# Attention without a turn back to tokens: two heads per column group, inverse sums spread by DMA, engine turns reordered

## The reference, cut to what matters

```python
x = x + L1_attn(layernorm(x), ...)        # x: 32 sequences, 256 tokens, 128 wide
# inside, HEADS = 16, HEAD_DIM = 8:
q = (h @ Wq.T + bq).reshape(b, s, 16, 8) * 8 ** -0.5
k = (h @ Wk.T + bk).reshape(b, s, 16, 8)
v = (h @ Wv.T + bv).reshape(b, s, 16, 8)
scores = einsum('bqhd,bkhd->bhqk', q, k)
probs  = softmax(scores, axis=-1)
out = einsum('bhqk,bkhd->bqhd', probs, v).reshape(b, s, 128)
return out @ Wo.T + bo
```

## Time and profile before

| | us |
|---|---|
| median of 3 runs (lowest, highest) | 1351.31 (1344.29, 1352.7) |
| the profiled execution, its own time | 1346.88 |
| its span in the trace | 1345.1 |
| attention phase: first M unit to last `add_y` | 633 to 1168 |
| PE, DVE, ACT, POOL busy over the whole span | 77%, 57%, 48%, 55% |
| DMA packets, MB | 92931, 104.74 |

### The profile page before, as it was taken

One profiled execution on the slowest core, in us unless ns is written; L12 is line 12 of the kernel. 1 busy time (PEld: TensorE's weight loads), 2 busy tenths in 40 slices (PEclk: granted clock), 3 DMA queues, 4 the chain that ended last, 5 costly groups with the idle time before them and its releaser, 6 DMA issues. The chain is left out here.

```text
span 1345.1 us, 31339 instructions
## 1 busy us (share of the span) xinstructions
PE 1032.9 (77%) x9288; PEld 732.2 (54%) x9289; DVE 763.8 (57%) x1576; ACT 647.5 (48%) x1294; POOL 745.8 (55%) x1517
## 2 busy tenths in 40 slices
PE   5688889568877776744899999999999999513455
PEld 4577777357854444432566666666666666302143
DVE  4466666363432222212677777777777777245982
ACT  4455555211212222212677777777777777402212
POOL 4455555245523333336667777777777775373312
PEclk9899999578999899985899999999999999856787
DMA  4700000301111111134333444444444443110000
GB/s 159 287 0 0 0 0 1 105 30 41 41 41 53 48 56 52 51 95 136 102 109 112 129 127 123 118 123 130 123 119 120 121 127 108 45 35 28 1 1 16
DMA packets 92931, 104.74 MB, mean 78 GB/s; under 512 B 11199, under 2 KB 76735, under 8 KB 92491
## 3 DMA queue, kind: packets, MB, share of 16 engines
q1 hardware_dynamic: 85530, 82.73, 21.6%
q0 software_dynamic: 5760, 11.68, 2.7%
q10 hardware_dynamic: 1584, 9.60, 1.8%
HBM read 62.48 MB, written 40.67 MB: 77 GB/s over the span
## 5 line engine op out<-in xcount | busy, mean ns | idle before, releaser
L1223 DVE TENSOR_REDUCE a_neg_max<-a_slot 128x4 f32<-128x1024 f32 x256 | 312.1, 1222 | 133.9 <-PE a_slot L1364 127.0
L1312 ACT ACTIVATE a_pT<-a_slot 128x1024 f32<-128x1024 f32 x256 | 257.8, 1020 | 83.3 <-PE a_slot L1378 78.4
L1378 PE MATMUL a_slot<-a_q_stack,a_k_stack 75*128 75x256 bf16 x1024 | 155.2, 274 | 17.7 <-ACT a_pT L1312 12.0
L1364 PE MATMUL a_slot<-a_k_stack,a_q_stack 72*128 72x256 bf16 x1024 | 157.5, 277 | 6.6 <-DMA a_k_stack<-part_dram 6.0
L661 POOL DMA_INDIRECT y_rows<-m_total,m_token x80 | 76.8, 960 | 137.3 <-ACT m_total L791 121.4
L1393 PE MATMUL a_ps_o<-a_pT,a_v_pad 128*32 128x256 f32 x2048 | 139.2, 385 | 0.0
L311 DVE TENSOR_TENSOR r_score<-ps_score,r_decay 128x512 f32<-128x512 f32 x128 | 85.0, 687 | 71.2 <-PE ps_score L442 67.8
L1364 PEld LDWEIGHTS a_slot<-a_k_stack,a_q_stack 72*128 72x128 bf16 x1024 | 90.8, 99 | 58.4 <-issue 31.0
L1378 PEld LDWEIGHTS a_slot<-a_q_stack,a_k_stack 75*128 75x128 bf16 x1024 | 92.3, 97 | 54.6 <-DVE a_neg_max L1223 41.3
L852 PE MATMUL m_banks<-expert_up,m_xeT 128*128 x160 | 82.9, 642 | 49.8 <-issue 39.4
L754 DVE COPY m_same<-m_banks 128x512 f32<-128x512 f32 x40 | 27.7, 692 | 140.7 <-PE m_banks L860 108.7
...
## 6 DMA issues: line engine op xcount, KB each, us to landing
...
part_dram<-a_part SPq DMA_DIRECT2D x64, 64.0 KB, 2.1
x_rows<-x SPq DMA_DIRECT2D x32, 128.0 KB, 3.6
```

Source lines behind the costliest of these rows:

```text
L1223: nc.vector.tensor_reduce(neg_max[:, p, half, t, g * UNIT:(g + 1) * UNIT], slots[SLOT_OF["m", j]][:], AX.X, ALU.max, negate=True).then_inc ...
L1312: nc.scalar.activation(pT[:, j % PT_RING], slots[SLOT_OF["e", j]][:], ACT.Exp).then_inc(e_read, 1)
L1364: ins = nc.tensor.matmul(slots[SLOT_OF["m", j]][:, q], q_stack[0:QK_ROWS, p, half, head, t * P:(t + 1) * P], k_stack[0:QK_ROWS, p, half, h ...
L1378: ins = nc.tensor.matmul(slots[SLOT_OF["e", j]][:, q], k_stack[0:EXP_ROWS, p, half, head, t * P:(t + 1) * P], q_stack[0:EXP_ROWS, p, half, ...
```

## The change

Heads 2j and 2j+1 share a column group of 32 columns: each has 16 (v, ones, zeros), and all four matmuls (two heads, two token tiles) add into one PSUM area, so that all 16 heads fit in the 128 partitions of two halves. ACT copies both halves in one operation (`copy_o`, lag 5). The output is never turned to tokens. Instead SP collects the 8 x 512 sums into [128, 32] (`collect_sums`), DVE inverts them (`invert`), SP stores them in DRAM (`store_inv`) and reads them back so that each row is spread over its 16 partitions (`spread_inv`, 256 KB), DVE multiplies (`normalise`, [128, 512], both inputs in SBUF), and `output` multiplies with a wo padded to the same layout, twice two matmuls instead of two. The bias bo goes into row 8 of that wo, where the input is a sum times its inverse; `bias` goes. The turns of all engines are reordered.

```diff
-        v_pad = m.sbuf("a_v_pad", [P, 2, TPS, AH, APAD])
+        v_pad = m.sbuf("a_v_pad", [P, 2, TPS, AH // SHARE, SHARE * SHARE, APART])
...
+            sp.wait_ge(preset_v, 3)
+            sp.dma_start(wo[AD:AD + 1, 0], bo[AD:AD + 1]).then_inc(ones_in, 16)
...
+            def collect_sums(s, p, r):
+                after(sp, o_copied, s + 1)
+                size = 2 * HALVES * S
+                sp.dma_start(o_inv[:, p], bass.AP(o_sums[:].tensor, o_sums[AD:, p].offset,
+                                                  [[size * APART, P // APART], [SUMS, APART], [1, SUMS]])
+                             ).then_inc(sums_in[p], 16)
+
+            def store_inv(s, p, r):
+                after(sp, inv_done, s + 1)
+                sp.dma_start(inv_dram[p].rearrange("k (i n) -> (k i) n", n=SUMS), o_inv[:, p]).then_inc(inv_stored[p], 16)
+
+            def spread_inv(s, p, r):
+                after(sp, inv_stored[p], twice(8, r + 1))
+                sp.dma_start(o_scale[:, p], inv_dram[p].unsqueeze(1).to_broadcast([P // APART, APART, HALVES * S])
+                             ).then_inc(scale_in[p], 16)
...
-            pipeline(sp, [(fill(1), 3), (store_x, 8), (give_max(1), 4), (store_parts, 2),
-                           (fill(0), 2), (give_max(0), 3), (store_out, 8)], B, ROUNDS)
+            pipeline(sp, [(fill(1), 3), (store_x, 8), (give_max(1), 4), (collect_sums, 5), (store_parts, 2), (fill(0), 2),
+                          (give_max(0), 3), (store_inv, 5), (spread_inv, 5), (store_out, 8)], B, ROUNDS)
...
-            def bias(s, p, r):
...
-            pipeline(pool, [(split_max(1), 4), (add_given, 0), (split_qk, 2), (bias, 2), (inv_std3, 7),
-                           (pad_v, 3), (split_max(0), 3), (inv_std, 0), (weigh, 7)], B, ROUNDS)
+            pipeline(pool, [(split_max(1), 4), (inv_std3, 7), (split_qk, 2), (add_given, 0), (pad_v, 3), (split_max(0), 3),
+                            (inv_std, 0), (weigh, 7)], B, ROUNDS)
...
-            def normalise(t):
...
+            def normalise(s, p, r):
+                after(dve, scale_in[p], 16 * (r + 1))
+                after(dve, y_done, s - 1)
+                nc.vector.tensor_tensor(oT[:, p], o_sums[:, p], o_scale[:, p], ALU.mult).then_inc(oT_done, 1)
+
+            def invert(s, p, r):
+                after(dve, sums_in[p], 16 * (r + 1))
+                nc.vector.reciprocal(o_inv[:, p], o_inv[:, p]).then_inc(inv_done, 1)
...
+            pipeline(dve, [(maximum(0), 3), (add_up, 8), (maximum(1), 3), (normalise, 6), (maximum(2), 3), (maximum(3), 3),
+                           (add_y, 6), (given_added, 0), (maximum(4), 3), (stats_of, 0), (settle, 0), (y_is_added, 6),
+                           (maximum(5), 3), (moments, 0), (stats3_of, 6), (settle3, 6), (maximum(6), 3), (moments3, 6),
+                           (invert, 5), (maximum(7), 3)], B, ROUNDS)
...
-            pipeline(act, [e[0], e[1], (copy_maxT(1), 4), (copy_o(1), 5), (copy_hT, 1), e[2], e[3], (copy_qk, 1),
-                           (norm3, 7), e[4], e[5], (copy_maxT(0), 3), (copy_o(0), 4), e[6], (copy_v, 1), (norm, 0),
-                           e[7], (copy_oT, 5)], B, ROUNDS)
+            pipeline(act, [e[0], e[1], (copy_maxT(1), 4), (copy_o, 5), (copy_hT, 1), e[2], e[3], (norm3, 7), e[4],
+                           (copy_qk, 1), e[5], (copy_maxT(0), 3), e[6], (copy_v, 1), e[7], (norm, 0)], B, ROUNDS)
...
                             half, turn = g // SHARE, g % SHARE
+                            ins = nc.tensor.matmul(ps_o[q * APAD:(q + 1) * APAD, half],
+                                                   v_pad[:, p, t, half * UNIT + q, turn * SHARE:(turn + 1) * SHARE],
+                                                   pT[:, (2 * g + t) % PT_RING, q], start=t == 0 and turn == 0,
+                                                   stop=t == TPS - 1 and turn == SHARE - 1, skip_group_check=True)
...
-            def by_token(t):
...
-            def transpose_o(s, p, r):
...
                 for t in range(TPS):
-                    ins = nc.tensor.matmul(ps_misc[:, t * D:(t + 1) * D], oT[:, p, t * P:(t + 1) * P], wo[:],
-                                           start=True, stop=True)
+                    for half in range(HALVES):
+                        ins = nc.tensor.matmul(ps_misc[:, t * D:(t + 1) * D], oT[:, p, half, t * P:(t + 1) * P],
+                                               wo[:, half], start=half == 0, stop=half == HALVES - 1)
...
-            pipeline(pe, [M[0], (output, 6), E[0], M[1], E[1], (transpose_max(1), 4), (values(3), 5), M[2],
-                           (transpose_h, 1), E[2], (by_token(0), 5), M[3], E[3], (project_qk, 1), (values(0), 4), M[4],
-                           E[4], (by_token(1), 5), M[5], E[5], (values(1), 4), (transpose_max(0), 3), M[6], E[6],
-                           (project_v, 1), M[7], E[7], (transpose_o, 5), (values(2), 4)], B, ROUNDS)
+            pipeline(pe, [M[0], E[0], M[1], E[1], (transpose_max(1), 4), (values(3), 5), M[2], (transpose_h, 1), E[2],
+                           M[3], E[3], (output, 6), (values(0), 4), M[4], E[4], (project_qk, 1), M[5], E[5],
+                           (values(1), 4), (transpose_max(0), 3), M[6], E[6], (project_v, 1), M[7], E[7],
+                           (values(2), 4)], B, ROUNDS)
```

More of the change, by code:

```diff
@@ L897 @@
 AG = AH // 4
+SHARE = 2
+APART = APAD // SHARE
 ROUNDS = 10
@@ L1020, in attention_phase @@
         o_copied = m.sem("a_o_copied")
-        otok_done = m.sem("a_otok_done")
+        sums_in = [m.sem(f"a_sums_in{i}") for i in range(2)]
         inv_done = m.sem("a_inv_done")
-        otok_copied = m.sem("a_otok_copied")
+        inv_stored = [m.sem(f"a_inv_stored{i}") for i in range(2)]
+        scale_in = [m.sem(f"a_scale_in{i}") for i in range(2)]
         oT_done = m.sem("a_oT_done")
-        oT_copied = m.sem("a_oT_copied")
         y_done = m.sem("a_y_done")
@@ L1254, in settle3 @@
             def settle3(s, p, r):
+                after(dve, ve3_done, 2 * (s - 1))
                 after(dve, stats3_part, TPS * (s + 1))
@@ L1264, in add_up @@
                 nc.vector.tensor_reduce(w_tok[:, bass.ds(s * TPS, TPS)], product[:, p], AX.X, ALU.add).then_inc(w_done, 1)
-            pipeline(dve, [(maximum(0), 3), (add_y, 6), (given_added, 0), (maximum(1), 3), (y_is_added, 6),
-                           (stats_of, 0), (maximum(2), 3), (settle, 0), (normalise(0), 5), (stats3_of, 6), (settle3, 6),
-                           (maximum(3), 3), (moments3, 6), (moments, 0), (maximum(4), 3), (normalise(1), 5),
-                           (maximum(5), 3), (add_up, 8), (maximum(6), 3), (maximum(7), 3)], B, ROUNDS)
+            pipeline(dve, [(maximum(0), 3), (add_up, 8), (maximum(1), 3), (normalise, 6), (maximum(2), 3), (maximum(3), 3),
+                           (add_y, 6), (given_added, 0), (maximum(4), 3), (stats_of, 0), (settle, 0), (y_is_added, 6),
+                           (maximum(5), 3), (moments, 0), (stats3_of, 6), (settle3, 6), (maximum(6), 3), (moments3, 6),
+                           (invert, 5), (maximum(7), 3)], B, ROUNDS)
         @block.scalar
@@ L1313, in exponential, with copy_o @@
                 return step
-            def copy_o(half):
-                def step(s, p, r):
-                    after(act, o_done, AG * s + 2 * half + 2)
-                    after(act, otok_done, TPS * s)
-                    nc.scalar.copy(oT_pad[:, 2 * half:2 * half + 2], ps_o[:]).then_inc(o_copied, 1)
-                return step
-            def copy_oT(s, p, r):
-                after(act, oT_done, s + 1)
-                after(act, y_done, s - 1)
-                nc.scalar.copy(oT[:, p], ps_misc[:, 0:S]).then_inc(oT_copied, 1)
+            def copy_o(s, p, r):
+                after(act, o_done, AG * (s + 1))
+                after(act, oT_done, s - 1)
+                nc.scalar.copy(o_sums[:, p], ps_o[:]).then_inc(o_copied, 1)
             def norm3(s, p, r):
@@ L1387, in step @@
                         after(pe, v_padded, s + 1)
[L1388 to L1389 removed]
+                        after(pe, o_copied, s)
                     after(pe, e_read, M_UNITS * s + 2 * g + 2)
@@ L1434, in transpose_max @@
                 return step
-            def by_token(t):
-                def step(s, p, r):
-                    if t == 0:
-                        after(pe, o_copied, HALVES * (s + 1))
-                    misc_free(f"token{t}", s)
-                    for g in range(AG):
-                        ins = nc.tensor.transpose(ps_misc[:, g * P:(g + 1) * P], oT_pad[:, g, t * P:(t + 1) * P],
-                                                  ident[:])
-                    ins.then_inc(otok_done, 1)
-                return step
             def project_qk(s, p, r):
@@ L1458, in project_v @@
                 ins.then_inc(v_done, 1)
-            def transpose_o(s, p, r):
-                after(pe, otok_copied, TPS * (s + 1))
-                misc_free("oT", s)
-                for t in range(TPS):
```

(10 more changed lines are left out.)

68 lines of the change are left out of this document (28 added, 40 removed).

## The result

The changed kernel takes 1368.5 us (median of 4 runs, 1364.4 to 1371.3); the kernel before takes 1349.2 (median of 4, 1344.3 to 1352.7). The ratio is 1.0143, 95% interval 1.0099 to 1.0187: slower by 1.4%. The forecast was 1371, in a range of 1350 to 1388.

What follows compares the result with a forecast made beforehand. PE was taken as the fullest engine; after the change, the add_given cycle plus lock sets 16.9 us a round. Loop 15.6, written-out rounds 0.8, start 0.7, end 4.5: +21.6 on some 1349, forecast 1371, range 1350 to 1388.

Steps and rivals of the forecast that it cites:

- The cycle through `add_given`: Attention loop: DVE's maximum(4) waits for POOL's late add_given, so a round cannot be shorter than 16.3 us.
- rival B: Loop: the add_given wait costs nothing because DVE is late anyway; PE's 15.7 us stands, about 1339 us; chance 0.09.
- PE alone would run at 16.2 - 0.8 + 0.25: Loop: PE's round after 0.8 us less matmul and transpose work and 0.25 more slot waits, 15.7 us.
- The lock: Loop: DVE's normalise, with two SBUF inputs, and POOL's operations block each other, making the round 16.9 us.
- 0.62 on the cycle: Loop: POOL's next operation waits for normalise, 0.69 less a 0.07 pause, adding 0.62 us to the add_given cycle.
- Rival A: Loop: no lock, POOL's short operations are not held up; round 16.3 us, 1355 us in all; chance 0.22.
- The DMA chain: Loop: cycle from maximum(6) through inverses, store, spread load, normalise and PE, 16.5 us with the lock, hidden below 16.9.
- Rival C: Loop: slower store and load make the DMA chain bind at 18.0 us a round; 1406 us, at half excess 1388; chance 0.16.
- The written-out rounds: Four attention rounds before the loop, priced at 0.2 us more each, +0.8 us.
- The end: From the last values(3) to add_y nothing hides the new DMA chain: 12.8 us for 7.7, net +4.5.
- the last three rounds 0: Last three attention rounds after the loop: they have no add_given, so they cost 0 us more.
- both fit: Loop: the later stack loads, fill(1) and fill(0), still arrive in time for PE within a 16.9 us round.

Runs made afterwards that it cites:

- e12: Changed kernel with PE's and ACT's turns refilled and invert and store_inv earlier, POOL's order kept: 1.0013 of the kernel before, 16.19 us a round.
- e6: Changed kernel with POOL's split_qk and add_given ahead of inv_std3, PE's and ACT's turns refilled, invert and store_inv earlier: 1303.9 us, 0.9790 of the kernel before.
- e11: Changed kernel with only PE's turns (values(3), transpose_max(1) ahead of E1, output ahead of E3) and ACT's reordered: 1.0115 of the kernel before, 16.38 us a round.
- e8: Changed kernel with e5's POOL and DVE order plus e11's PE and ACT turns: 0.9930 of the kernel before, 15.55 us a round.
- e3: Changed kernel with normalise multiplying by ones without waiting for the spread inverses, DMAs still issued: 1.0049 of the kernel before, 16.41 us a round.
- e5: Changed kernel with POOL's split_qk and add_given ahead of inv_std3, DVE awaiting add_given after maximum(4): 1.0119 of the kernel before, 16.38 us a round.
- e9: Changed kernel with e5's POOL and DVE order plus invert and store_inv earlier, PE's turns kept: 0.9987 of the kernel before, 16.14 us a round.
- e2: Changed kernel with normalise replaced by a same-size operation reading one SBUF tensor, waits kept: 1.0120 of the kernel before, 16.21 us a round.
- e1: Changed kernel with add_given moved ahead of inv_std3 and split_qk on POOL: 1392.5 us, 1.0369 of the kernel before.

## Why the prediction was right, and where it was not

The direction, the size and the main mechanism were right. The single terms were not, and they made up for each other: that the sum is within 0.5 us is luck.

**The cycle through `add_given`**: right. The stations stand within 0.3 us of their forecast, and e12 against e6 and e11 against e8 show that this order costs 0.93 and 0.83 us a round once the others are out of the way. It was not the only limit, though. Without the wait for the spread the round is 16.41 (e3), without that for `add_given` 16.38 (e5), and with neither 16.14 (e9), where PE's in-order waits at E1 and E3 are left. So opening one cycle alone gains 0.2 us, and the next limit is less than 0.5 us away. That answers for rival B too: its claim that DVE is late anyway is wrong, and so is its 15.7 us for PE alone. With the change's order PE reached 16.14, 0.4 more than the forecast's step "PE alone would run at 16.2 - 0.8 + 0.25"; the 15.55 of e8 are those of another PE order. (The "1.4 us of a round" that the prediction calls waits don't fit its own window either: PE is busy for 96.1% of 16.2 us, which leaves 0.6. No term rests on it.)

**The lock**: right in kind, too large. The mis-sized term is "0.69 less the 0.07 that POOL pauses anyway, 0.62 on the cycle". It was 0.36 on POOL, on the mean of the rounds, and 0.39 on the round (e2). The reason given, that the row shows a full block, is right. But a block ends 0.14 before the recorded end of the operation in its way. So `normalise` gets on 0.14 before the recorded end of POOL's operation and lets POOL on 0.14 before its own: 0.69 - 0.08 - 2 x 0.14 = 0.33. The prediction's own row had it: DVE's operation of 1.23 ended 1.1 after POOL's, not 1.23. That explains 22 x (0.62 - 0.36) = 5.7 of the 6.1 us by which the loop term was over. Rival A (no lock) is excluded by e2 and by these rows. The Trainium skill ("SBUF — State Buffer", Who interferes with whom) says that the one that comes second blocks until the first is done, and the trace agrees, up to those 0.14 us.

**The DMA chain**: its loop forecast of 16.5 is not contradicted, but no run has this chain as the only limit. With `add_given` out of the way (e5) the round is 16.38, where `normalise` still waits 8.3 us in all for a_o_scale; taking that wait away as well gains 0.24 (e9). The parts: the load was issued 1.45 us after the store (908.16 to 909.61), not 2.15, and `normalise` went on 4.28 after that, not 3.35; together 5.7 for 5.5. The pieces of 128 bytes did not lengthen the store: over the 32 of them it landed in 1.7 us (median, 1.4 to 3.3) where 2.1 was forecast. (The 512 bytes that the prediction takes from the Trainium skill stand in "DMA: Bandwidth & Descriptors" under Specifications, not in the section it names.) Rival C (18 us a round) is excluded: without the wait the round is shorter by 0.2. Its price was also added up wrongly: 18.0 less 16.9 is 1.1 us a round, so 27 rounds give some 1401 us, not 1406. And with both DMAs at their upper bounds the cycle is 19.1 only without the lock's wait, which the 16.5 beside it includes.

**The written-out rounds**: forecast +0.8, measured -1.6. The cycle was priced there as in the loop, but three of these rounds are shorter than before by 0.7 to 1.8 us; why was not tried and stays open. The one that is longer by 2.4 has PE waiting 1.47 us for the load of the stacks, and the lower clock behind it.

**The end**: forecast +4.5, measured +14.0, and e3 shows that the wait for the spread is the cause. The failing step is "the last three rounds 0". Their `add_given` is indeed gone, but so is the work that hid the chain. The last stretch was priced well. The last `values(3)` ends at 1176.19 + 2.25 = 1178.44, 11.65 before `add_y`; before, 1160.27 + 1.07 = 1161.34, 6.59 before it. That is 5.1 of the 14.0, for a forecast of 4.5. The other 8.9 are in the rounds ahead of it, among them the gaps of 2.60 (to 1133.18) and 2.88 at E3 and the half clock after the second.

**The stack load**, "both fit": true in the loop, where PE waits for it twice in 21 rounds (0.8 us), and thin. e1 used up the slack with 0.7 us, and in one written-out round it did not fit.
